# Two small parameter loads of a fused transformer kernel, fetched as single rows and spread to the partitions by TensorE

## The chip, the core and the metric

The kernel runs on one core of one Trainium2 chip. The metric is the device time of one execution in microseconds (us). The core has five instruction streams that matter here: TensorE (PE, with its weight loads shown apart as PEld), VectorE (DVE), ScalarE (ACT), GpSimd (POOL) and SyncE (SP). Every stream runs in order and is tied to the others by semaphores. SP and ACT also issue DMA transfers, which 16 DMA engines carry out; in the profile SP's queue is q1 and ACT's is q10.

## What is computed

Two layers over x of shape (4, 256, 256) and a context of shape (4, 256, 128). Each layer adds a gated cross attention and then a gated feed-forward part:

```python
x = x + tanh(g_xattn[0]) * L0_xattn(layernorm(x), ctx)      # the part that the change touches
x = x + tanh(g_ffn[0])   * L0_ffn(layernorm(x))             # ternary weights, 8-bit activations
x = x + tanh(g_xattn[1]) * L1_xattn(layernorm(x), ctx)      # 16 heads
x = x + tanh(g_ffn[1])   * L1_ffn(layernorm(x))             # 64 experts, top 8

def L0_xattn(logits, features):
    query = features @ Wq.T + bq                            # bq, bk: 128 values each
    key = features @ Wk.T + bk
    attention = softmax(query @ key.T)
    return attention-weighted sum of logits
```

`bq` and `bk` are the first layer's biases. The four values of `g_xattn` and `g_ffn` are the gates. All of them are float32.

## The kernel before

The 1024 tokens lie as 8 tiles of 128, or as 4 batches of 256. Everything fits in SBUF, the order of the work is written out by hand for each engine, and a tile of one batch moves from engine to engine by semaphores. The first layer's attention goes through these functions, all within the first 40 us:

- SP issues the loads in the order of lines 302 to 321: the transposed context `ctxT_raw` (512 KB), the weights `wqk0` (128 KB; the profile prints `wqk`), `x` in two halves of 512 KB, the gate weights, and so on.
- ACT issues two loads at its start: `bqk` (line 1582, 128 partitions of 8 bytes) and `gains_raw` (line 1583, 128 partitions of 16 bytes; the host has copied the four gates into 128 rows). Both count on semaphore `l_small`.
- PE begins with `warm()` (lines 748 to 753): eight matmuls of a matrix of ones into PSUM bank 4 that nobody reads, then waits for `ctxT_raw` and `wqk0`. `query_key` (line 744) follows four times: one float32 matmul 128x128 by 128x512 each, which the profile shows as two passes, so that line 744 has eight. `energy` (line 759) multiplies query and key of a batch, `turn_rows_0` (723) and `turn_att` (767) transpose, `mix` (777) applies the attention.
- ACT copies each `query_key` result from PSUM to `qkA` with the bias added (`copy_qk`, line 1385; it waits for `l_small` in the first call), and `gates()` (line 1555) takes the tanh of the gates between the third and the fourth copy. Then come the exponentials (`exp_A`, 1391).
- DVE begins with `stats_0` (lines 1880 and 1883) on the first half of x, then takes the row maxima of the energies (`max_A`, line 1906), and normalises the exponentials (`norm_A`, 1910 and 1912).
- POOL writes the constants, splits the context (`low_ctxT`, 566), and normalises x (516).

`hs` is a scratch tile of the first feed-forward part. Its first writer is `abs_gate` (line 1559). PSUM bank 3 is first used by `energy(2, 3)`. `sum_abs` (line 784) is a later stage of PE with matmuls that load a full 128x128 float32 weight and stream one column.

Of the kernel before, what the change touches and what calls it, by code (L numbers as in the profile page):

```python
# [9 lines left out]
ACT = mybir.ActivationFunctionType  # L10
AX = mybir.AxisListType

P = 128
# [24 lines left out]
def flamingo_kernel(nc, x_tok, ctx_tok, ctxT, qk0, bias0, gains, gate_wT, down_wT, down_tail,  # L38
                    norm_g1, norm_g2, gqk, head_qk, head_vo, router_w, expert_w, shared_w,
                    shared_down, outT, w_rows):  # L40
    with ExitStack() as ctx:
        def sb(name, shape, dt=F32):
            return ctx.enter_context(nc.sbuf_tensor(name, shape, dt))

        def sem(name):
            return ctx.enter_context(nc.semaphore(name))

        pairs = [ctx.enter_context(nc.psum_tensor(f"bank{2 * i}", [P, 2, 512], F32)) for i in range(4)]
        bank = [pairs[i // 2][:, i % 2, :] for i in range(8)]
# [8 lines left out]
        ones = sb("ones", [P, P])  # L58
# [6 lines left out]
        ctxT_lo = sb("ctxT_lo", [P, TOK], F32R)  # L65
        ctx_hi = sb("ctx_hi", [P, TILES, CDIM], F32R)
        ctx_lo = sb("ctx_lo", [P, TILES, CDIM], F32R)
        gains_raw = sb("gains_raw", [P, 4])
        tg = sb("tg", [P, 4])
        spare = sb("spare", [P, 1])  # L70

# [5 lines left out]
        xnT_hi = sb("xnT_hi", [P, KH, TOK], F32R)  # L77
        xnT_lo = sb("xnT_lo", [P, KH, TOK], F32R)

        bqk = sb("bqk", [P, 2])  # L80
        nmA = sb("nmA", [P, BATCH, 2])
        sumA = sb("sumA", [P, BATCH, 2])
        invA = sb("invA", [P, BATCH, 2])
# [43 lines left out]
        l_ctxT, l_ctx, l_qk0, l_small = (sem(n) for n in ("l_ctxT", "l_ctx", "l_qk0", "l_small"))  # L127
# [5 lines left out]
        l_exp = [sem(f"l_exp{i}") for i in range(4)]  # L133
        pool_const = sem("pool_const")
        g_ctx = sem("g_ctx")
        a_ctx, a_tg = sem("a_ctx"), sem("a_tg")

        v_link = sem("v_link")
# [10 lines left out]
        def link_g(pool, ins):  # L149
# [11 lines left out]
        t_qkA, a_qkA, t_eA, v_mA, a_eA, v_nA, t_aA, a_aA, t_oA, v_xA = (sem(n) for n in (  # L161
            "t_qkA", "a_qkA", "t_eA", "v_mA", "a_eA", "v_nA", "t_aA", "a_aA", "t_oA", "v_xA"))
# [6 lines left out]
        def sf(name, shape, dt=F32):  # L169
            return bctx.enter_context(nc.sbuf_tensor(name, shape, dt))  # L170
# [13 lines left out]
        hs = sf("hs", [P, 4, INTER])  # L184
# [2 lines left out]
        hT = sf("hT", [P, 2, KI, P], BF16)  # L187
        down_t = sf("down_t", [P, KI, HID], BF16)
        bctx.close()
        silu_g, h_raw = hs[:, 0:2, :], hs[:, 2:4, :]  # L190
        flat = w2[:, :, :].rearrange("p i n -> p (i n)")
        qkA = flat[:, 0:2 * TOK].rearrange("p (i n) -> p i n", i=2)
# [82 lines left out]
        def bank4(i):  # L275
            return bank[i][:, :].rearrange("p (a n) -> p a n", a=2)
# [440 lines left out]
        def _(pe):  # L717
# [29 lines left out]
            def warm():  # L747
                pe.wait_ge(pool_const, 2)
                for _ in range(8):
                    pe.matmul(bank[4][:, 0:P], ones[:, :], ones[:, :], start=True, stop=True)  # L750
                pe.wait_ge(pool_const, 5)
                pe.wait_ge(l_ctxT, 16)
                pe.wait_ge(l_qk0, 16)
# [226 lines left out]
            def experts_down(par, slot, t, s, start=False):  # L980
# [5 lines left out]
                mm.then_inc(t_D, 1)  # L986

            warm()
            query_key(0, 0, 2)
            query_key(1, 0, 5)  # L990
# [380 lines left out]
        def _(act):  # L1371
# [9 lines left out]
            def copy_qk(i, h, k, bk):  # L1381
                act.wait_ge(t_qkA, k + 1)
                if k == 0:
                    act.wait_ge(l_small, 32)
                act.activation(qkA[:, i, h * 512:(h + 1) * 512], bank[bk][:, :], ACT.Identity,
                               bias=bqk[:, i:i + 1]).then_inc(a_qkA, 1)

            def exp_A(b, bk):
                act.wait_ge(v_mA, b + 1)
# [159 lines left out]
            def high_ctxT():  # L1549
                act.wait_ge(l_ctxT, 16)  # L1550
                act.activation(ctxT_hi[:, :], ctxT_raw[:, :], ACT.Copy).then_inc(a_ctx, 1)

            def gates():
                act.wait_ge(l_small, 32)
                act.activation(tg[:, :], gains_raw[:, :], ACT.Tanh).then_inc(a_tg, 1)

            def abs_gate(k):
                act.wait_ge(l_gate[k], 16)
# [20 lines left out]
            def load_table(function):  # L1579
                act.activation(spare[:, :], tg[:, 0:1], function)  # L1580

            act.dma_start(bqk[:, :], bias0).then_inc(l_small, 16)
            act.dma_start(gains_raw[:, :], gains).then_inc(l_small, 16)
            high_ctxT()
            copy_qk(0, 0, 0, 2)
            copy_qk(1, 0, 1, 5)
            copy_qk(0, 1, 2, 7)
            gates()
            copy_qk(1, 1, 3, 2)
            exp_A(0, 6)  # L1590
# [283 lines left out]
        def _(dve):  # L1874
            T = tinyB

            def tile_stats(i0, i1):

                for i in range(i0, i1):
                    ins = dve.bn_stats(stats[:, i, :], x[:, i, :])  # L1880
                link(dve, ins)
                for i in range(i0, i1):
                    ins = dve.bn_aggr(mv[:, i, :], stats[:, i, :])
                return ins
# [15 lines left out]
            def stats_0(b):  # L1900
                dve.wait_ge(l_x[b // 2], 16)
                tile_stats(2 * b, 2 * b + 2).then_inc(v_pw1, 1)

            def max_A(b, bk):
                dve.wait_ge(t_eA, b + 1)
                dve.tensor_reduce(nmA[:, b, :], bank4(bk), AX.X, ALU.max, negate=True).then_inc(v_mA, 1)
# [269 lines left out]
            def key_gain():  # L2176
                dve.wait_ge(l_gqk, 16)
                dve.tensor_scalar(gk[:, :], gqk_raw[:, 0:1], gqk_raw[:, 1:2], float(D) ** -0.5, ALU.mult,
                                  ALU.mult).then_inc(v_gk, 1)

            stats_0(0)
            stats_0(1)
            max_A(0, 6)
            max_A(1, 1)
            max_A(2, 3)
            norm_A(0)
            stats_0(2)
# [411 lines left out]
```

## Time and profile before

| | before |
|---|---|
| median of 3 runs | 620.29 us |
| lowest, highest | 620.06, 620.79 us |
| the profiled execution's own time | 620.25 us |
| its span, first to last instruction | 618.5 us |
| outside the span | 1.75 us |
| PE, PEld, DVE, ACT, POOL busy | 98, 85, 78, 68, 38% of the span |

The profile is of one execution. Times in it count from the start of its span. A row of the timeline gives start, duration, engine, line, operation, tiles and shapes, and in square brackets how long the engine had been idle and what released it. A PE row's duration goes from the start of a pass to its modelled end, and passes overlap, so that the distance between two starts is what a pass costs in a row of passes. The chain of work that ended last is followed back from the last instruction, each piece to what released it.

### The profile page before, as it was taken

To read this page: it belongs to the slowest core of one execution; us is meant where nothing else is said; L and a number is where in the kernel's file an instruction comes from. 1 tells how busy PE (TensorE), PEld (TensorE's weight loads), DVE (VectorE), ACT (ScalarE), POOL (GpSimd) and SP (SyncE) were. 2 spreads that over 40 slices of the span, in tenths; PEclk is the share of its full clock that TensorE was granted. 3 is DMA by queue.
4 is the path that set the end of the run, shared out by engine and by line. 5 is a ranking of instruction groups with operands and counts; after the bars stand their busy time and mean duration, and the time that the engine had idled before them with its cause. 6 is when DMAs were issued, how large, how long until landed. Compare 5 with 4: busy or idle time off the path is not lost.

```text
span 618.5 us, 11618 instructions
## 1 busy us (share of the span) xinstructions
PE 605.6 (98%) x3644; PEld 524.2 (85%) x3644; DVE 482.0 (78%) x1139; ACT 422.2 (68%) x1080; POOL 233.8 (38%) x280
## 2 busy tenths in 40 slices
PE   8889999999999999999999999999999999999997
PEld 6657899999999999999998888888887888887886
DVE  4999889888777687788775787778877677777776
ACT  6998998988888888889898444364444444443442
POOL 5899798666666666556662020000000000000000
PEclk9999999999999999999999999999999999999999
DMA  8503221000000000000030445443756466554630
GB/s 294 198 26 103 78 77 37 17 1 2 2 2 2 2 2 2 1 2 1 6 125 2 140 159 147 150 149 100 214 166 171 113 171 166 165 154 148 199 128 34
DMA packets 33653, 56.47 MB, mean 91 GB/s; under 512 B 12800, under 2 KB 13504, under 8 KB 33600
## 3 DMA queue, kind: packets, MB, share of 16 engines
q1 hardware_dynamic: 33312, 55.82, 29.6%
q8 instruction: 26, 0.43, 0.3%
q14 instruction: 27, 0.22, 0.1%
q10 hardware_dynamic: 288, 0.00, 0.0%
HBM read 53.45 MB, written 1.31 MB: 89 GB/s over the span
## 4 chain that ended last, share of the span: by engine, by line
PE 87%; DVE 6%; issue 2%; POOL 2%; ACT 2%; DMA 1%; SPq 0%; DVEq 0%; ACTq 0%; POOLq 0%
PE bank L296 24%; PE bank L298 24%; PE bank L297 24%; PE bank L897 4%; PE bank L872 2%; PE bank L864 2%; PE bank L938 1%; PE bank L824 1%; ACT att L1489 1%; DVE hs L1974 1%; PE bank L817 1%; DMA wqk<-in_qk 1%; PE bank L797 1%; PE bank L744 1%; PE bank L777 1%
## 5 line engine op out<-in xcount | busy, mean ns | idle before, releaser
L1537 ACT ACTIVATE inter_hi<-inter 128x512 fp32r<-128x512 f32 x63 | 39.8, 632 | 140.6 <-DVE inter L2165 140.6
L296 PE MATMUL bank<-xnT_hi,front_hi 128*128 128x512 f32 (+1 forms) x260 | 102.0, 392 | 0.0
L298 PE MATMUL bank<-xnT_hi,front_lo 128*128 128x512 f32 (+1 forms) x260 | 101.7, 391 | 0.0
L297 PE MATMUL bank<-xnT_lo,front_hi 128*128 128x512 f32 (+1 forms) x260 | 101.7, 391 | 0.0
L2169 DVE TENSOR_TENSOR inter_lo<-inter,inter_hi 128x512 fp32r<-128x512 f32 x63 | 43.6, 692 | 37.5 <-ACT inter_hi L1537 37.0
L1489 ACT ACTIVATE att<-bank,shift,rq 128x256 f32<-128x256 f32 x128 | 71.3, 572 | 1.9 <-DVE shift L2055 1.9
L557 POOL TENSOR_TENSOR att<-att,rowinv 128x512 f32<-128x512 f32 x60 | 62.9, 1064 | 12.1 <-DVE rowinv L2065 12.1
L2138 DVE TENSOR_TENSOR prod<-gate_s,bank 128x512 f32<-128x512 f32 x63 | 43.2, 686 | 22.0 <-PE bank L298 20.0
L2048 DVE TENSOR_REDUCE rowmax<-bank 128x2 f32<-128x512 f32 x64 | 43.5, 684 | 20.7 <-PE bank L298 20.3
L297 PEld LDWEIGHTS bank<-xnT_lo,front_hi 128*128 128x128 f32 x260 | 48.9, 188 | 11.3
L298 PEld LDWEIGHTS bank<-xnT_hi,front_lo 128*128 128x128 f32 x260 | 48.8, 188 | 11.3
L296 PEld LDWEIGHTS bank<-xnT_hi,front_hi 128*128 128x128 f32 x260 | 48.8, 188 | 11.1
L541 POOL TENSOR_TENSOR rk<-msq,minus_half 128x4 f32<-128x4 f32 x32 | 32.8, 1024 | 67.3 <-DVE msq L2037 67.3
L296 PE MATMUL bank<-inter_hi,front_hi 128*128 128x512 f32 (+1 forms) x130 | 51.2, 394 | 0.0
L297 PE MATMUL bank<-inter_lo,front_hi 128*128 128x512 f32 (+1 forms) x130 | 51.0, 392 | 0.0
L298 PE MATMUL bank<-inter_hi,front_lo 128*128 128x512 f32 (+1 forms) x130 | 51.0, 392 | 0.0
L2165 DVE TENSOR_TENSOR inter<-prod,w_all 128x512 f32<-128x512 f32 x63 | 43.6, 692 | 3.6 <-DVE prod L2138 1.8
L2060 DVE TENSOR_TENSOR attT_lo<-bank,attT_hi 128x512 fp32r<-128x512 f32 x64 | 43.1, 681 | 3.3 <-ACT attT_hi L1478 2.9
L296 PE MATMUL bank<-m_all,o_hi 128*128 128x256 f32 x128 | 38.9, 304 | 0.7 <-DVE o_lo L2075 0.6
L1478 ACT ACTIVATE attT_hi<-bank 128x512 fp32r<-128x512 f32 x64 | 35.6, 603 | 4.5 <-PE bank L897 4.4
L1533 ACT ACTIVATE gate_s<-bank 128x512 f32<-128x512 f32 x63 | 37.0, 587 | 2.2 <-PE bank L298 2.0
L296 PE MATMUL bank<-kh,qh 128*128 128x256 f32 x128 | 36.7, 287 | 0.1
(270 smaller groups left out, 1816.5 us busy)
## 6 DMA issues: line engine op xcount, KB each, us to landing
w_all<-w_rows SPq DMA_DIRECT2D x128, 128.0 KB, 2.9
raw<-in_expert_w SPq DMA_DIRECT2D x32, 384.0 KB, 3.5
wvo_raw<-in_expert_w SPq DMA_DIRECT2D x16, 384.0 KB, 3.6
e_more<-in_expert_w SPq DMA_DIRECT2D x16, 384.0 KB, 3.6
raw<-in_head_qk SPq DMA_DIRECT2D x8, 384.0 KB, 3.4
wvo_raw<-in_head_vo SPq DMA_DIRECT2D x4, 384.0 KB, 3.0
w_keep<-in_head_vo SPq DMA_DIRECT2D x4, 384.0 KB, 3.3
gate_raw<-in_gate_wT SPq DMA_DIRECT2D x2, 704.0 KB, 9.0
```

The lines of the kernel that those rows point to most:

```text
L296: pe.matmul(out, l_hi, r_hi_, start=start, stop=False, skip_group_check=True)
L297: pe.matmul(out, l_hi, r_lo_, start=False, stop=False, skip_group_check=True)
L298: return pe.matmul(out, l_lo, r_hi_, start=False, stop=stop, skip_group_check=True)
L557: pool.tensor_tensor(a, a, rowinv[:, n % 2, h, :].unsqueeze(2).broadcast_to([P, 2, SEQ]), ALU.mult).then_inc(g_att, 1)
L1489: act.activation(att[:, n % 2, h, t, :], bank4(SBK[h])[:, t, :], ACT.Exp, bias=shift[:, n % 2, h, t:t + 1], scale=rq[:, n % 4, t * 2 + h:t ...
L1533: act.activation(gate_s[:, slot, :], bank[GB][:, :], ACT.Silu).then_inc(a_silu, 1)
L1537: act.activation(inter_hi[:, slot, :], inter[:, slot, :], ACT.Copy).then_inc(a_Ihi, 1)
L2048: dve.tensor_reduce(rowmax[:, n % 2, h, :], bank4(SBK[h]), AX.X, ALU.max, negate=True).then_inc(v_max, 1)
L2060: dve.tensor_tensor(attT_lo[:, h, :, :], bank4(TBK[h]), f(attT_hi[:, h, :, :]), ALU.subtract).then_inc(v_Tlo, 1)
L2138: dve.tensor_tensor(prod[:, slot, :], gate_s[:, slot, :], bank[UB][:, :], ALU.mult).then_inc(v_mul1, 1)
L2165: dve.tensor_tensor(inter[:, slot, :], prod[:, slot, :], w_all[:, par, :], ALU.mult).then_inc(v_mul2, 1)
L2169: dve.tensor_tensor(inter_lo[:, slot, :], inter[:, slot, :], f(inter_hi[:, slot, :]), ALU.subtract).then_inc(v_Ilo, 1)
```

## The change

The biases are fetched as one row of 256 values into the first partition of `hs`, the gates as one row of four values behind it. PE gets three matmuls in `warm()`, behind the eight of ones and a wait for `l_small`: two take every second value of the bias row as weights of one partition by 128 columns and a single 1.0 as the moving operand, which puts 128 bias values into a column of bank 3; the third takes one partition of ones as weights and the four gates as the moving operand, which puts them into four columns of all partitions. DVE gets a copy of the six columns to a new tile `small` as its first instruction. ACT's `copy_qk` and `gates()` read `small` and wait for that copy by a new semaphore `v_small`.

```diff
-        gains_raw = sb("gains_raw", [P, 4])
+        small = sb("small", [P, 6])
-        bqk = sb("bqk", [P, 2])
+        t_small, v_small = sem("t_small"), sem("v_small")
+        bias_row, gain_row = hs[0:1, 0, 0:2 * P], hs[0:1, 0, 2 * P:2 * P + 4]
         (in warm, behind the eight matmuls of ones)
+                pe.wait_ge(l_small, 32)
+                for i in range(2):
+                    pe.matmul(bank[3][:, i:i + 1], bias_row.rearrange("o (p i) -> o i p", i=2)[:, i, :],
+                              ones[0:1, 0:1], start=True, stop=True, skip_group_check=True)
+                pe.matmul(bank[3][:, 2:6], ones[0:1, :], gain_row, start=True, stop=True,
+                          skip_group_check=True).then_inc(t_small, 1)
                 pe.wait_ge(pool_const, 5)
                 pe.wait_ge(l_ctxT, 16)
                 pe.wait_ge(l_qk0, 16)
         (in copy_qk)
                 if k == 0:
-                    act.wait_ge(l_small, 32)
+                    act.wait_ge(v_small, 1)
                 act.activation(qkA[:, i, h * 512:(h + 1) * 512], bank[bk][:, :], ACT.Identity,
-                               bias=bqk[:, i:i + 1]).then_inc(a_qkA, 1)
+                               bias=small[:, i:i + 1]).then_inc(a_qkA, 1)
         (in gates)
-                act.wait_ge(l_small, 32)
-                act.activation(tg[:, :], gains_raw[:, :], ACT.Tanh).then_inc(a_tg, 1)
+                act.wait_ge(v_small, 1)
+                act.activation(tg[:, :], small[:, 2:6], ACT.Tanh).then_inc(a_tg, 1)
         (ACT's first two instructions)
-            act.dma_start(bqk[:, :], bias0).then_inc(l_small, 16)
-            act.dma_start(gains_raw[:, :], gains).then_inc(l_small, 16)
+            act.dma_start(bias_row, bias0.rearrange("(o p) i -> o (p i)", o=1)).then_inc(l_small, 16)
+            act.dma_start(gain_row, gains[0:1, :]).then_inc(l_small, 16)
         (DVE)
+            def keep_small():
+                dve.wait_ge(t_small, 1)
+                dve.tensor_copy(small[:, :], bank[3][:, 0:6]).then_inc(v_small, 1)
+            keep_small()
             stats_0(0)
```

## Rows read from the trace of the kernel before

**Rows 1.** The page: busy time of each engine, the granted clock by slices, the chain.
```profile
PE 605.6 (98%) x3644; PEld 524.2 (85%) x3644; DVE 482.0 (78%) x1139; ACT 422.2 (68%) x1080; POOL 233.8 (38%) x280
PEclk9999999999999999999999999999999999999999
PE 87%; DVE 6%; issue 2%; POOL 2%; ACT 2%; DMA 1%; SPq 0%; DVEq 0%; ACTq 0%; POOLq 0%
```

**Rows 2.** The chain that ended last, first 14 us: start us, us, piece.
```profile
0.73 0.40 SPq L302
1.18 4.05 DMA wqk<-in_qk
5.23 0.14 issue
5.37 3.90 PE bank L744 x8
9.27 2.60 PE bank L759 x12
11.89 0.69 DVE nmA L1906
```

**Rows 3.** The timeline of 0 to 6.8 us, the engines' rows around the change.
```profile
1.14 3.78 PE L750 MATMUL bank<-ones 128*128 128x128 f32 x16 [1.14 <-POOL minus_magic L437]
...
4.92 1.06 ACT L1551 ACTIVATE ctxT_hi<-ctxT_raw 128x1024 fp32r<-128x1024 f32 x1 [1.98 <-DMA ctxT_raw<-in_ctxT]
...
5.37 3.90 PE L744 MATMUL bank<-ctxT_raw,wqk 128*128 128x512 f32 x8 [0.45 <-DMA wqk<-in_qk]
...
6.73 0.69 ACT L1385 ACTIVATE w<-bank,bqk 128x512 f32<-128x512 f32 x1 [0.75 <-PE bank L744]
```

**Rows 4.** Timeline of PE from 4.5 us, of PEld from 5 us.
```profile
4.50 0.42 PE L750 MATMUL bank<-ones 128*128 128x128 f32 x1
```
```profile
5.34 0.50 PEld L744 LDWEIGHTS bank<-ctxT_raw,wqk 128*128 128x128 f32 x2 [0.72 <-issue]
6.10 0.19 PEld L744 LDWEIGHTS bank<-ctxT_raw,wqk 128*128 128x128 f32 x1 [0.26 <-issue]
6.53 0.19 PEld L744 LDWEIGHTS bank<-ctxT_raw,wqk 128*128 128x128 f32 x1 [0.24 <-issue]
```

**Rows 5.** Timeline, one float32 matmul of one column (two passes) and its neighbours.
```profile
21.97 0.30 PEld L784 LDWEIGHTS bank<-absum,ones 128*128 128x128 f32 x2
...
22.08 0.28 PE L784 MATMUL bank<-absum,ones 128*128 128x1 f32 x2
22.22 1.19 PE L931 MATMUL bank<-ctxT_hi 128*128 128x512 f32 x4
```

**Rows 6.** DMA issues at the start: size each, us from issue to landing.
```profile
ctxT_raw<-in_ctxT SPq DMA_DIRECT2D x1, 512.0 KB, 4.2
...
bqk<-in_bias ACTq DMA_DIRECT2D x1, 1.0 KB, 4.0
gains_raw<-in_gains ACTq DMA_DIRECT2D x1, 2.0 KB, 4.2
```

**Rows 7.** Timeline: the issue of the second small load; queue q10, 2 to 5 us.
```profile
1.18 0.45 ACTq L1583 DMA_DIRECT2D gains_raw<-in_gains x1
```
```profile
q10 hardware_dynamic: 288, 0.00, 5.3%
```

**Rows 8.** Busy time by stretch: PE, PEld, DVE, ACT, POOL, then PEclk, DMA share, GB/s.
```profile
3.00:3.50 0.50, 0.50 (x4) 0.50 (x4) 0.00 (x0) 0.00 (x0) 0.00 (x0) 1.00 0.79 287
...
8.00:9.00 1.00, 1.00 (x3) 0.39 (x3) 0.91 (x4) 0.83 (x2) 0.49 (x1) 1.00 1.02 425
...
30.00:40.00 10.00, 7.55 (x48) 5.68 (x49) 9.79 (x20) 8.96 (x23) 8.08 (x9) 1.00 0.14 41
...
60.00:618.50 558.50, 553.42 (x3356) 486.12 (x3356) 432.92 (x1019) 371.00 (x975) 186.55 (x203) 1.00 0.28 84
```

**Rows 9.** Timeline, 8 to 14 us: who holds up DVE and PE there.
```profile
8.05 0.75 DVE L1880 BATCH_NORM_STATS2 stats<-x 128x6 f32<-128x256 f32 x2 [8.05 <-DMA x<-in_x_tok]
...
9.76 0.25 DVE L1883 BATCH_NORM_AGGREGATE mv<-stats 128x2 f32<-128x6 f32 x2
...
10.17 0.69 DVE L1906 TENSOR_REDUCE nmA<-bank 128x2 f32<-128x512 f32 x1 [0.16 <-PE bank L759]
...
13.36 0.66 PE L767 MATMUL bank<-ident,w 128*128 128x128 f32 x4 [1.03 <-DVE w L1912]
```

**Rows 10.** Timeline: a DVE instruction on a PSUM column; ACT's first use of loaded gate weights.
```profile
18.12 0.16 DVE L1955 TENSOR_SCALAR wsc<-bank 128x1 f32<-128x1 f32 x1 [0.27 <-PE bank L784]
```
```profile
14.55 1.42 ACT L1559 ACTIVATE hs<-gate_raw 128x1408 f32<-128x1408 f32 x1
```

## The prediction

> **What bounds the kernel now.** I read the page first. PE is busy 98% of the span and holds 87% of the chain [rows 1], so that nothing outside PE's order is worth much by itself. The change, however, touches only the first 10 us. There the question is not which engine is busiest but which wait ends last. The chain in order of time answers that [rows 2]: it starts with SP's issues, rides on the transfer of `wqk` until 5.23 us, enters PE with `query_key` (line 744, 3.90 us), goes on with `energy` (line 759) and reaches DVE's maxima at 11.89 us. The small loads are not on it. ACT's first bias copy began at 6.73 us because PE had finished its matmul then, not because the bias came [rows 3].
>
> Next I looked at what happens if the start slips or comes forward. From 30 to 40 us DVE is busy 9.79 of 10 us, and behind 60 us PE is busy 553.42 of 558.50 us [rows 8]. No transfer times the stages behind the start: ACT's `abs_gate` at 14.55 us shows no idle time before it [rows 10]. So I take it that a shift of `query_key` goes into the end one to one, and that it is the only thing that can.
>
> **The change part by part.** The sum is made against the profiled execution, 620.25 us with 618.5 us of span; it lies 0.04 us under the median of the three runs (620.29), so no correction is needed.
>
> (1) *The loads.* `bqk` and `gains_raw` are issued at 0.74 and 1.18 us and land 4.0 and 4.2 us later [rows 6, 7], at 4.7 and 5.4 us. ACT's queue shows 288 packets which took 5.3% of 16 engines' time over the 3 us from 2 to 5 us [rows 7], which is 0.16 us for each engine. That is the lower bound of what removing them frees. The upper bound comes from the rate: 287 GB/s while they are under way, 425 GB/s later [rows 8]. The 640 KB of `ctxT_raw` and `wqk0` at 425 GB/s need 1.5 us, at 287 they need 2.2 us, so `wqk` could land up to 0.7 us earlier if all of that difference were their doing (the start-up of the queues has its part in it, so I take 0.2 us). Both ends are worth nothing by themselves if PE isn't ready, see (3). The same holds for x: the first half starts DVE at 8.05 us, and DVE is through with its two statistics at 10.01 us and then waits 0.16 us for PE's energy [rows 9]. An earlier x only lengthens that wait.
>
> (2) *When the rows are there.* No transfer of one row is in the trace. The nearest are the small loads themselves. At the latest they land where the 128 packets of the second did, 1.18 + 4.2 = 5.38 us; at the earliest only the issue time, 1.2 us, is a firm limit. With one data packet in place of 128 a row has hardly any turns to wait for beside the big transfers, and I take both to be landed before 4.5 us, when PE starts its last pass of ones [rows 4].
>
> (3) *PE's three matmuls.* This is the term that decides. They stand in front of `query_key` in PE's order. Each float32 matmul is two passes, so six passes, each with a weight load of 128 columns, though only one partition is filled. The 16 passes of ones go from 1.14 to 4.50 us, start of first to start of last: 3.36 / 15 = 0.224 us a pass [rows 3, 4]. This is the lower clock level: a pass of 512 columns later takes 0.43 us (6.10 to 6.53) [rows 4], so 128 columns should cost 0.107 at the 2.4 GHz level and 0.213 at 1.2 GHz. (The granted clock in the rows prints 1.00 from the start [rows 8]; I go by the durations.) At the high level a matmul of one column costs 0.07 a pass hidden behind others (22.08 to 22.22 us for two) and 0.15 by its loads (0.30 for two) [rows 5]. For six passes that gives 0.42 us at the least, 0.9 us at the high level by the loads, and 1.34 us at 0.224. The clock is still low at 4.7 us, so I take 0.224, the nearest row in time and in weight shape. The last pass of ones gives way at 4.50 + 0.22 = 4.72 us, and `query_key` starts at 4.72 + 1.34 = 6.07 us in place of 5.37.
>
> The Trainium skill speaks on this in "TensorE: Matmul & The Clock Gate", section "LDWEIGHTS (loading the stationary operand)": the time of a weight load goes with its columns and not with the rows filled, 128 columns at 1.2 GHz or 107 ns. That is a rule against this change, since using one partition saves nothing. With its figure the six passes would be 0.64 us, `query_key` would start at 5.36 us and the change would cost nothing, as an estimate from the page; the trace has 0.15 to 0.22 us for a float32 load and decides.
>
> (4) *What of that is given back by the clock.* Before, the first pass of line 744 lasts from 5.37 to 6.10 us, where the next ones take 0.43 [rows 4]. At half speed it would need 0.85. So the clock rose within it: with t us at half speed, t/0.85 + (0.73 - t)/0.43 = 1 gives t = 0.6, a rise at about 5.98 us. If it rises at the same moment, the late `query_key` runs at full speed from its first pass. Its second pass starts at 6.07 + 0.43 = 6.50 us in place of 6.10: a delay of 0.40 us, not 0.70.
>
> (5) *The hop over DVE.* The last small pass ends at about 5.84 + 0.25 = 6.1 us, then a DVE instruction on a few PSUM columns takes 0.16 us [rows 10]; with a hand-over on either side `small` is there at 6.4 us. ACT needs it when the first `query_key` is through, 6.73 + 0.40 = 7.1 us. DVE has nothing queued behind the new wait that could run before x lands at 8.05 us [rows 9]. So the hop costs nothing, with 0.7 us of cover on ACT and 1.6 us on DVE; if the small matmuls ended later, `query_key` would move with them and the cover on ACT would stay.
>
> (6) *ACT's issues* remain two, its table load and its wait for the context until 4.92 us [rows 3] hide them. The copy of the bias reads as many bytes as before. All this is zero.
>
> Sum: -0.0 (loads, hidden behind PE) + 0.40 (PE) + 0 (DVE, ACT) = +0.4 us; 620.25 + 0.4 = 620.65, rounded to 620.7 us. The bounds of (3) and (2): with 0.42 us for the six passes `query_key` starts at 5.14 us if the transfer is early enough, runs its first pass at half speed up to the rise (0.84 of the 0.85 us that it needs), and its second starts at 5.99 us: 0.11 us early, giving 620.1. With the rows landing at 5.38 us, the passes begin there, 2.7 of them at 0.224 up to 5.98 us and 3.3 at 0.15, end at 6.48 us, and the second pass of `query_key` comes at 6.91: +0.81, giving 621.1 us.
>
> **The rivals.**
> *The clock rises later (slower).* Before, PE streams full columns from 1.14 us to 4.92, pauses 0.45 us and streams 512 columns until the clock rises near 5.98 us. After, the 1.3 us ahead of that moment hold six weight loads and a dozen moving columns. If this little work keeps the clock down, `query_key` runs at 1.2 GHz from 6.07 us. Each pass costs 0.43 us more; if all eight are slow, 8 x 0.43 = 3.4 us on top of 0.4, 624.1 us. A rise at 9 us costs (9.0 - 6.07) / 2 = 1.5 us, 620.25 + 0.4 + 1.5 = 622.1 us. It turns into slower by over 0.2% when the rise comes later than about 7.7 us: 0.4 + (7.7 - 6.07) / 2 = 1.2. For it speaks that the passes of one column leave the array empty between the loads. Against it speaks that the engine had worked without a break for 3.8 us by then and no longer pauses for 0.45 us, and that PE's wait of 1.03 us at 13.36 us did not bring the clock down: four passes of 128 columns took 0.66 us right behind it [rows 9]. The Trainium skill, same page, section "The HAM clock gate" has activity release the clock and idleness take it back; taken by itself it would have the filled pause help, and no row here shows how a weight load counts. Chance 12%.
> *The transfers were what held the start (faster).* If the small packets cost the two big transfers 0.7 us and the six passes are cheap, `query_key` can start at 5.14 us as above: 620.1 us, a gain, but one within 0.2%. Even if the clock rose with it and all passes came 0.23 us early, it would be 620.0 us. PE's passes of ones end where they do, so that the idle time of 0.45 us is all there is. For more, something behind 60 us would have to fall differently; no row shows what. Chance of a gain over 0.2%: 7%.
> *It doesn't do what it says.* If the row is cut into pieces again or the landing is governed by the big transfers of the other queue, the rows come no earlier than 5.4 us: 621.1 us by the bound above. Part of the forecast's range, 15%.
>
> **How the numbers follow.** A difference of 0.2% is 1.24 us here, about what a measurement of this kernel can tell from no change. My forecast with its bounds (620.1 to 621.1) has 66% and the late rows 15%, both within 0.2%: same 0.81. Slower is the clock rival, 0.12. Faster is the rest, 0.07. The range takes the lower bound of 620.1 less a little for the spread of the runs (620.06 to 620.79), 619.9, and at the upper end reaches into the clock case up to a rise at 9 us, 622.1.
>
> **What would show it.** In the new profile I look for six passes of `warm`'s new lines between 4.7 and 6.1 us without a wait for a DMA before them; the first pass of line 744 near 6.07 us, its distance to the next 0.43 us; DVE's maximum at 10.6 in place of 10.17 us with 0.5 us of idle time before it, released by PE; POOL's and DVE's statistics at 8.0 us or a little sooner; ACT's first bias copy still released by PE and not by DVE. The forecast is wrong if PE waits for the small rows, if the second pass of line 744 still takes 0.7 us or more, if the six passes together take under 0.6 us, or if a slip at 10 us is no longer seen at 60 us.

## The result: two groups of executions, 1.0024 of the time before

| | before | after |
|---|---|---|
| executions | 20 | 19 |
| median | 620.30 us | 622.66 us |
| lowest, highest | 619.88, 621.06 us | 620.45, 623.31 us |
| ratio after / before | | 1.0024, 95% interval 1.0015 to 1.0033 |
| the profiled execution and its span | 620.25, 618.5 us | 622.66, 620.9 us |

(One execution of the changed kernel, of 744.99 us, and one of e4 below, of 852.26 us, had a mean granted clock of 0.755 and 0.656 and are left out; one of e3, of 621.81 us with 0.948, is counted.) The median says little here, because nothing lies near the middle: nine executions are at 620.45 to 620.93 us and ten at 622.66 to 623.31 us. The profiled one is of the upper group. By the ratio the change costs 1.5 us.

The page of the changed kernel, busy time of the engines, answers to [rows 1]:

```profile
PE 608.4 (98%) x3650; PEld 526.2 (85%) x3650; DVE 482.4 (78%) x1140; ACT 422.0 (68%) x1080; POOL 233.8 (38%) x280
```

The chain that ended last, first 15 us (start us, us, piece), answers to [rows 2]. The transfer of `wqk` is gone from it. Behind POOL's constants it runs in PE's own order:

```profile
1.14 3.78 PE bank L751 x16
4.92 0.94 PE bank L754 x4
5.86 0.43 PE bank L756 x2
6.29 5.11 PE bank L745 x8
11.40 2.60 PE bank L766 x12
14.03 0.69 DVE nmA L1917
```

Line 745 is `query_key` (744 before), 5.11 us in place of 3.90. Its weight loads in the timeline of PEld, each of which begins when the pass before the one it serves begins, answer to [rows 4]:

```profile
4.85 0.92 PEld L754 LDWEIGHTS bank<-ones,hs 1*128 1x128 f32 x4 [0.23 <-issue]
5.66 0.54 PEld L756 LDWEIGHTS bank<-hs,ones 1*128 1x128 f32 x2
6.21 0.50 PEld L745 LDWEIGHTS bank<-ctxT_raw,wqk 128*128 128x128 f32 x2
7.23 0.34 PEld L745 LDWEIGHTS bank<-ctxT_raw,wqk 128*128 128x128 f32 x1 [0.52 <-issue]
8.08 0.34 PEld L745 LDWEIGHTS bank<-ctxT_raw,wqk 128*128 128x128 f32 x1 [0.52 <-issue]
8.94 0.34 PEld L745 LDWEIGHTS bank<-ctxT_raw,wqk 128*128 128x128 f32 x1 [0.52 <-issue]
9.52 0.19 PEld L745 LDWEIGHTS bank<-ctxT_raw,wqk 128*128 128x128 f32 x1 [0.25 <-issue]
9.95 0.19 PEld L745 LDWEIGHTS bank<-ctxT_raw,wqk 128*128 128x128 f32 x1 [0.24 <-issue]
```

The passes are 0.85 us apart (7.23, 8.08, 8.94), then once 0.58, then 0.43. So the array ran at 1.2 GHz up to a moment between 8.94 and 9.52. With t us of that pass at half speed, t/0.85 + (0.58 - t)/0.43 = 1 gives t = 0.3: the clock rose at 9.24 us. The trace's own record of the granted clock begins at the same 9.24 us; ahead of its first entry the page prints 1.00. In the profile of before this record begins at 5.83 us, a little ahead of the 5.98 of the prediction. There the first pass of line 744 was counted from 5.37 us, but the weight load for the second pass, which begins with the first pass, starts at 5.51. From 5.51 to 6.10 us the same sum is t/0.85 + (0.59 - t)/0.43 = 1 with t = 0.32, and gives 5.83 too.

DVE and ACT behind it, from the timeline, answer to [rows 9] and [rows 3]:

```profile
6.32 0.17 DVE L1913 COPY small<-bank 128x6 f32<-128x6 f32 x1 [6.32 <-PE bank L756]
8.23 0.75 DVE L1887 BATCH_NORM_STATS2 stats<-x 128x6 f32<-128x256 f32 x2 [1.75 <-DMA x<-in_x_tok]
8.33 0.69 ACT L1392 ACTIVATE w<-bank,small 128x512 f32<-128x512 f32 x1 [2.63 <-PE bank L745]
12.30 0.69 DVE L1917 TENSOR_REDUCE nmA<-bank 128x2 f32<-128x512 f32 x1 [2.11 <-PE bank L766]
```

The first maximum starts at 12.30 us in place of 10.17, +2.13 us. `energy` starts 2.14 us later (first the row of before, then the changed kernel's):

```profile
9.10 2.75 PE L759 MATMUL bank<-w 128*128 128x256 f32 x12
```

```profile
11.24 2.75 PE L766 MATMUL bank<-w 128*128 128x256 f32 x12
```

VectorE's instruction at the end of the first layer, line 1904 (1897 before), starts at 61.65 in place of 59.49 (+2.16), and the whole execution takes 2.41 us more. Before and after:

```profile
59.49 0.67 DVE L1897 TENSOR_TENSOR xnT_lo<-bank,xnT_hi 128x512 fp32r<-128x512 f32 x1
```

```profile
61.65 0.67 DVE L1904 TENSOR_TENSOR xnT_lo<-bank,xnT_hi 128x512 fp32r<-128x512 f32 x1
```

### The profile page after: what moved, and what is told of

It reads as the page before. It is cut to its first block, busy times and chain, and to the rows that moved or that the text cites. A ratio compares the mean times of both kernels' runs of the same rounds, so it can differ in the third digit from the quotient of the medians.

```text
span 620.9 us, 11631 instructions
## 1 busy us (share of the span) xinstructions
PE 608.4 (98%) x3650; PEld 526.2 (85%) x3650; DVE 482.4 (78%) x1140; ACT 422.0 (68%) x1080; POOL 233.8 (38%) x280
## 4 chain that ended last, share of the span: by engine, by line
PE 89%; DVE 6%; ACT 2%; issue 2%; POOL 1%; ACTq 0%; DVEq 0%; POOLq 0%
PE bank L297 24%; PE bank L298 24%; PE bank L299 24%; PE bank L904 4%; PE bank L879 2%; PE bank L871 2%; ACT att L1496 1%; PE bank L945 1%; PE bank L831 1%; PE bank L745 1%; DVE hs L1985 1%; PE bank L824 1%; PE bank L804 1%; PE bank L784 1%; PE bank L751 1%
```

## The experiments

Each table row counts executions; before was run beside them on the same chip. The first four (e1 for the first time, e2, e3 and e4) ran on one chip, all later ones on another, on which before itself has more upper executions. "Upper" are those of 621.5 us and more. The ratio is that to before.

| kernel | all | upper | values of the others | values of the upper | ratio, 95% interval |
|---|---|---|---|---|---|
| before, with the result | 20 | 0 | 619.88 to 621.06 | | |
| before, beside the first four | 35 | 1 | 619.70 to 620.95 | 622.90 | |
| before, beside the second four | 35 | 6 | 619.96 to 621.49 | 622.13 to 622.61 | |
| before, beside the last four | 34 | 4 | 619.99 to 621.14 | 622.04 to 622.82 | |
| changed, with the result | 19 | 10 | 620.45 to 620.93 | 622.66 to 623.31 | 1.0024, 1.0015 to 1.0033 |
| changed, again | 12 | 5 | 620.28 to 621.01 | 622.81 to 623.10 | 1.0018, 1.0005 to 1.0031 |
| e1, both times | 23 | 0 | 618.86 to 621.41 | | 1.0007 and 0.9983, see below |
| e2 | 11 | 4 | 620.01 to 620.65 | 622.30 to 622.75 | 1.0010, 0.9997 to 1.0023 |
| e3 | 12 | 5 | 620.38 to 620.93 | 621.81 to 623.57 | 1.0025, 1.0013 to 1.0036 |
| e4 | 10 | 0 | 619.97 to 621.14 | | 1.0005, 0.9996 to 1.0014 |
| e5 | 12 | 8 | 620.11 to 620.59 | 622.36 to 622.79 | 1.0011, 0.9997 to 1.0025 |
| e6 | 12 | 7 | 619.90, 621.14 to 621.37 | 621.50 to 622.75 | 1.0013, 1.0003 to 1.0023 |
| e8 | 12 | 5 | 619.39 to 620.11 | 621.67 to 622.31 | 0.9996, 0.9982 to 1.0010 |
| e10 | 11 | 1 | 619.66 to 620.85 | 621.73 | 0.9998, 0.9989 to 1.0007 |
| e11 | 11 | 0 | 619.21 to 621.00 | | 0.9998, 0.9989 to 1.0007 |
| e12 | 11 | 7 | 621.12 to 621.47 | 621.55 to 622.65 | 1.0020, 1.0011 to 1.0029 |

A profile shows one execution, and here it is often an end of a group: it is the fastest of its kernel in e1 (both times), e3, e6, e11 and the second run of the changed kernel, and the slowest in e2 and e5.

### Which half of the change: e1 and e2

e1, the loads alone:

```diff
-                pe.wait_ge(l_small, 32)
-                (the three small matmuls)
-                dve.wait_ge(t_small, 1)
-                dve.tensor_copy(small[:, :], bank[3][:, 0:6]).then_inc(v_small, 1)
+                dve.wait_ge(l_small, 32)
+                dve.memset(small[:, :], 0.5).then_inc(v_small, 1)
```

> The change's loads alone: biases and gates are fetched as rows, PE has none of the three small matmuls, and VectorE fills the six columns with 0.5 once the rows have landed, so the real biases and gates are left out of the computation. Theory (the clock): in the changed kernel's profile the first three passes of the projection lie 0.85 us apart and later ones 0.43, so the clock rose near 9.2 us in place of 5.98, because of what PE does from 4.85 to 6.2 us. Without the small matmuls PE is as before: all executions near 620.3 us, none at 622 to 623, the weights landing 0.2 us earlier than 5.23 us at most. Rival (the loads shift something else, for instance which transfer comes first): executions at 622 to 623 us here too.

Measured: 620.27 us, ratio 1.0007 (0.9998 to 1.0015), eleven executions between 619.22 and 621.41, none at 622. This is as the theory of the clock expects; the loads alone bring no upper group, which the rival wanted. The weights landed 3.5 us after their issue, at 4.7 us, 0.5 earlier than before where 0.2 was expected. The values spread more than expected.

e2, the matmuls alone, in the kernel before:

```diff
                 for _ in range(8):
                     pe.matmul(bank[4][:, 0:P], ones[:, :], ones[:, :], start=True, stop=True)
+                for _ in range(2):
+                    pe.matmul(bank[3][:, 0:1], ones[0:1, :], ones[0:1, 0:1], start=True, stop=True)
+                pe.matmul(bank[3][:, 0:4], ones[0:1, :], ones[0:1, 0:4], start=True, stop=True)
```

> The loads as before (256 small packets), and behind the eight matmuls of ones three more of the same shapes as the change's, one partition of weights by 128 columns with 1, 1 and 4 moving columns, of ones and read by nobody. The clock theory expects what the changed kernel shows: executions in two groups, near 620.7 and near 622.9 us, and in a profile of the slower group passes of the projection 0.85 us apart up to about 9.2 us. The rival that the loads bring the slower group expects 620.7 us alone.

Measured: two groups, seven at 620.01 to 620.65 us and four at 622.30 to 622.75. The profile fell into the upper one (622.75 us) and shows the same picture as the changed kernel, in PEld's timeline:

```profile
6.21 0.50 PEld L744 LDWEIGHTS bank<-ctxT_raw,wqk 128*128 128x128 f32 x2
7.23 0.34 PEld L744 LDWEIGHTS bank<-ctxT_raw,wqk 128*128 128x128 f32 x1 [0.52 <-issue]
8.08 0.34 PEld L744 LDWEIGHTS bank<-ctxT_raw,wqk 128*128 128x128 f32 x1 [0.52 <-issue]
8.94 0.34 PEld L744 LDWEIGHTS bank<-ctxT_raw,wqk 128*128 128x128 f32 x1 [0.52 <-issue]
9.64 0.19 PEld L744 LDWEIGHTS bank<-ctxT_raw,wqk 128*128 128x128 f32 x1 [0.36 <-issue]
```

With all 256 packets in place, three matmuls that nobody reads are enough for the upper group, in 4 of 11 executions where before has 1 of 35 beside them.

### Is it the slip or what fills it: e4, e3, e5, e8

e4 is the kernel before with `range(11)` in place of `range(8)` in `warm()`.

> The kernel before with eleven full matmuls of ones in place of eight: the same six extra passes in front of the projection, all of 128 partitions by 128 columns. Clock theory: extra 6 x 0.224 us in front of the projection, the rise where it was, 5.9 us, the second pass of the projection at about 6.5 us in place of 6.10: +0.4 us, 620.7 us in all executions. Rival (the slip of the projection by itself, past 5.98 us, costs the slower group, whatever fills the time): two groups, 620.7 and 622.9 us.

Measured: one group, 619.97 to 621.14 us, median 620.56, ratio 1.0005 (0.9996 to 1.0014). The profile, 620.62 us, in PEld's timeline:

```profile
5.79 0.45 PEld L744 LDWEIGHTS bank<-ctxT_raw,wqk 128*128 128x128 f32 x2
6.47 0.19 PEld L744 LDWEIGHTS bank<-ctxT_raw,wqk 128*128 128x128 f32 x1 [0.24 <-issue]
6.90 0.19 PEld L744 LDWEIGHTS bank<-ctxT_raw,wqk 128*128 128x128 f32 x1 [0.24 <-issue]
```

The second pass is at 6.47 us (6.5 expected), 0.37 later than before, and the execution takes 0.37 us more. So in the profiles six full passes ahead of the projection cost 0.4 us as worked out; the ratio of 1.0005 agrees with that, but also with nothing.

e3 keeps the single partition and fills the columns:

```diff
-                    pe.matmul(bank[3][:, i:i + 1], ..., ones[0:1, 0:1], ...)
+                    pe.matmul(bank[3][:, i * P:(i + 1) * P], ..., ones[0:1, :], ...)
-                pe.matmul(bank[3][:, 2:6], ones[0:1, :], gain_row, ...)
+                pe.matmul(bank[3][:, 2 * P:3 * P] (as 32 by 4), ones[0:1, :], gain_row (32 times), ...)
```

> The changed kernel with 128 moving columns in each of the three small matmuls in place of 1, 1 and 4 (the ones and the gates repeated), still one partition of weights; VectorE copies in two pieces. If it is the few streamed columns that keep the clock down, the passes cost about the same 0.22 us each, the rise stays at 5.9 us, and all executions are near 620.7 us. If the single filled partition counts as little work as well, two groups stay, near 620.7 and 622.9 us.

Measured: seven at 620.38 to 620.93, four at 622.80 to 623.57 us and one at 621.81 between them. e5 is the other way round, in the kernel before:

```diff
+                for _ in range(3):
+                    pe.matmul(bank[3][:, 0:1], ones[:, :], ones[:, 0:1], start=True, stop=True)
```

> The kernel before, with three matmuls of ones of 128 partitions by 128 columns of weights and a single moving column each behind the eight: the same six passes, full in partitions, empty in columns. With one filled partition and 128 moving columns there were two groups of executions, with 128 by 128 one group. If the filled partitions decide, one group, 619.9 to 621.2 us. If both a single partition and a single column count as little work, two groups, the upper one near 622.7 us, in a third to a half of the executions.

Measured: four at 620.11 to 620.59, eight at 622.36 to 622.79 us. Its profile is of the upper group (622.79 us) and has the latest rise of all, at about 10.2 us, where the distance of the passes falls from 0.85 to 0.43:

```profile
5.78 0.55 PEld L744 LDWEIGHTS bank<-ctxT_raw,wqk 128*128 128x128 f32 x2
6.84 0.34 PEld L744 LDWEIGHTS bank<-ctxT_raw,wqk 128*128 128x128 f32 x1 [0.52 <-issue]
7.70 0.34 PEld L744 LDWEIGHTS bank<-ctxT_raw,wqk 128*128 128x128 f32 x1 [0.52 <-issue]
8.55 0.34 PEld L744 LDWEIGHTS bank<-ctxT_raw,wqk 128*128 128x128 f32 x1 [0.52 <-issue]
9.40 0.34 PEld L744 LDWEIGHTS bank<-ctxT_raw,wqk 128*128 128x128 f32 x1 [0.52 <-issue]
10.25 0.19 PEld L744 LDWEIGHTS bank<-ctxT_raw,wqk 128*128 128x128 f32 x1 [0.51 <-issue]
10.68 0.19 PEld L744 LDWEIGHTS bank<-ctxT_raw,wqk 128*128 128x128 f32 x1 [0.24 <-issue]
```

Here the projection started no later (5.85 us) than in e4 (5.99; the first weight load for it is at 5.78 and 5.79), and the clock still came late. e4 and e5 have the same passes with the same weights at the same times up to there and differ only in the moving columns, 128 against 1 (and in the PSUM bank that these write, 4 against 3), and they have 0 of 10 and 8 of 12 upper executions. That rules out the slip as the cause and leaves the columns. They ran on different chips; beside e5, before has 6 of 35, still far from 8 of 12. For the single partition the case is weaker: e3 with its five of twelve against e4's none of ten, on one chip, and e3 differs from e4 also by a short pause of the weight loads, see (3) below. e8 is the changed kernel with 128 partitions read, 127 of them zeros:

```diff
+            dve.memset(hs[:, 0, 0:2 * P + 4], 0.0).then_inc(v_small, 1)
+            act.wait_ge(v_small, 1)          (ahead of ACT's two loads)
-                    pe.matmul(bank[3][:, i:i + 1], (hs[0:1, ...]), ones[0:1, 0:1], ...)
+                    pe.matmul(bank[3][:, i:i + 1], (hs[:, ...]), ones[:, 0:1], ...)
                 (the third likewise; ACT's later waits for v_small count one more)
```

> The changed kernel with the rows' tile set to zero by VectorE ahead of the loads, and the three small matmuls taking all 128 partitions (127 of zeros) as weights, with 1, 1 and 4 moving columns. If the partitions read decide over the clock, one group near 620.7 us; if the values or the columns do, two groups as before, 620.7 and 622.9 us. The loads start some 0.3 us later, hidden behind the passes of ones.

Measured: seven at 619.39 to 620.11, five at 621.67 to 622.31 us; two groups, both nearly 1 us lower than expected (ratio 0.9996, 0.9982 to 1.0010). The profile has the weights at 1.18 + 3.4 = 4.6 us and the projection at 5.08. The changed kernel's own profile of the lower group (below) has the projection at 5.27, so that 0.2 us of the gain are there; why it does better by more than that wasn't followed up.

Together: of the kernels with the same six passes more than before (the changed one, e2, e3, e4, e5, e8), the one whose passes are full in partitions and columns has 0 of 10 in the upper group, the others 4 to 8 of 11 or 12 (the changed one 15 of 31). A dozen executions each don't rank the latter among themselves. No single one of e2 and e3 would prove the difference from e4 either; all together (37 of 78 against 0 of 10), and e5 by itself, do.

### Before or behind the rise: e6 and e12

e6 is the changed kernel with `range(6)` in `warm()`, e12 with `range(12)`.

> The changed kernel with six matmuls of ones ahead of the three small ones in place of eight, so that PE is through at 1.14 + 18 x 0.224 = 5.2 us. Clock theory: less full work ahead of the small passes, so the late rise comes in at least as many executions as in the changed kernel (11 of 20); the lower group moves from 620.7 to about 620.3 us, the upper from 622.9 to about 622.5. The rival that the slower group comes from the slip of the projection past 5.98 us expects the upper group to be gone.

Measured: 621.58 us, one execution at 619.90, nine at 621.14 to 621.93, two at 622.64 and 622.75. The rival falls, since leaving the slip out didn't take the later times away (where the projection started in them no profile shows); the two expected groups are not there either, the times fill the stretch between. The profile caught the 619.90, so the middle values have no profile. In it the clock rose during the small passes, at 4.63 us by its record: the weight loads are 0.21 us apart up to 4.54 and 0.11 from 4.71 us on. It also shows when the rows are there, in PEld's timeline:

```profile
4.15 0.74 PEld L754 LDWEIGHTS bank<-ones,hs 1*128 1x128 f32 x4 [0.39 <-DMA hs<-in_gains]
4.82 0.30 PEld L756 LDWEIGHTS bank<-hs,ones 1*128 1x128 f32 x2
5.13 0.30 PEld L745 LDWEIGHTS bank<-ctxT_raw,wqk 128*128 128x128 f32 x2
```

PE waited 0.39 us for the gates' row, until 4.15 us, of the 0.9 us (four passes at 0.224) that two fewer matmuls give. So e6 differs from the changed kernel by this pause too, and not only by the work ahead of the small passes.

> The changed kernel with twelve matmuls of ones ahead of the small ones in place of eight. Clock theory: a late rise needs the small passes to come before the clock has risen; with 24 full passes, up to 6.5 us at the lower level, it has risen by then in nearly all executions, and there is one group, at 621.0 to 622.0 us for the later start of the projection (7.2 to 7.4 us). The rival by which the slip of the projection itself brings the upper group expects all executions above 622.7 us.

Measured: one broad group, 621.12 to 622.65 us, median 621.67, three of eleven above the expected 622.0. No execution is where the rival wants all of them. The profile (621.18 us) has passes of 0.43 us from the start of the projection at 6.28 us:

```profile
5.49 0.54 PEld L754 LDWEIGHTS bank<-ones,hs 1*128 1x128 f32 x4
6.28 0.30 PEld L745 LDWEIGHTS bank<-ctxT_raw,wqk 128*128 128x128 f32 x2
6.81 0.19 PEld L745 LDWEIGHTS bank<-ctxT_raw,wqk 128*128 128x128 f32 x1 [0.24 <-issue]
```

Its clock rose at 4.28 us, as early as in other kernels without the four extra matmuls, so that the profile doesn't show what these do. The times say a little more: a rise at 9.24 us would put an execution near 621.18 + (9.24 - 4.28) / 2 = 623.7 us, as an estimate, and none lies there. So the upper group of the changed kernel seems to go when more full work stands ahead of the small passes, but the spread of 1.5 us isn't explained, and the time is worse all the same.

### What the loads alone are worth: e1 again, e10, e11

> The loads alone once more (real biases and gates left out, 0.5 in their place), for a second profile and for the lower group against the kernel before: 11 executions lay at 619.2 to 620.3 (6) and 620.9 to 621.4 us (5). If its lower group is real, it comes from the weights landing at 4.75 us in place of 5.23 and the projection starting 0.6 us earlier: lower values 0.5 us under those of before. If the upper group is a later rise of the clock, its profile, if it falls there, has passes of the projection 0.85 us apart past 6 us.

Measured: 619.93 us, twelve at 618.86 to 620.16, ratio 0.9983 (0.9973 to 0.9992). The profile (618.86 us), timeline of PEld and DVE, shows the projection 0.6 us and x 1.2 us earlier than before:

```profile
4.72 0.30 PEld L745 LDWEIGHTS bank<-ctxT_raw,wqk 128*128 128x128 f32 x2 [0.20 <-issue]
5.26 0.19 PEld L745 LDWEIGHTS bank<-ctxT_raw,wqk 128*128 128x128 f32 x1 [0.24 <-issue]
6.82 0.75 DVE L1881 BATCH_NORM_STATS2 stats<-x 128x6 f32<-128x256 f32 x2 [2.62 <-DMA x<-in_x_tok]
```

The first time the ratio was 1.0007, the second time 0.9983; the lowest values lie 0.5 and 1.1 us under those of before both times. The upper part of the first time (five at 620.9 to 621.4 us) didn't come back, so that it has no profile.

e10 has the packets, but behind the weights on SP's queue:

```diff
             sp.dma_start(wqk0[:, :, :], qk0).then_inc(l_qk0, 16)
+            sp.dma_start(bqk[:, :], bias0).then_inc(l_small, 16)
+            sp.dma_start(gains_raw[:, :], gains).then_inc(l_small, 16)
-            (the same two on ACT)
```

> The kernel before with the two small loads (256 packets, nothing on PE) issued by SyncE behind the projection's weights in place of by ScalarE beside them. If the small packets held the context and the weights up, these land at 4.7 to 4.8 us as with the rows alone, the projection starts at about 4.8 us, and the executions lie at 619.0 to 620.2 us as there. x comes later than with the rows (6.8 us), near 8 us, and that costs nothing. If what helped with the rows was something else, the executions lie as those of before (619.7 to 621).

Measured: 620.36 us, ratio 0.9998 (0.9989 to 1.0007): the weights land at 1.18 + 3.6 = 4.8 us as expected, the time doesn't follow. The profile shows two new waits, in ACT's waits and DVE's timeline:

```profile
ACT w L1387 <- DMA gains_raw<-in_gains: 1.0, 1, 1.0
```

```profile
9.53 0.25 DVE L1883 BATCH_NORM_AGGREGATE mv<-stats 128x2 f32<-128x6 f32 x2
9.70 1.32 DVE L1906 TENSOR_REDUCE nmA<-bank 128x2 f32<-128x512 f32 x2
```

ACT's first bias copy now waits 1.0 us for the gates, and x lands at 7.83 us, so that DVE is busy with statistics until 9.70 and takes the maxima without any wait for PE. The next bound lies 0.5 us behind the first. e11 below, where ACT has no such wait, runs into the same one: its first maximum starts at 9.74 us, right behind the statistics.

e11 puts biases and gates into one load of 128 packets of 24 bytes:

```diff
-            act.dma_start(bqk[:, :], bias0).then_inc(l_small, 16)
-            act.dma_start(gains_raw[:, :], gains).then_inc(l_small, 16)
+            act.dma_start(small[:, :], bias0).then_inc(l_small, 16)      (bias0 of 6 columns, from the host)
```

> The kernel before with biases and gates side by side in one load of 128 packets of 24 bytes, nothing on PE. Half the packets: if the cost is by packet, the weights land halfway, near 5.0 us, and the executions lie 0.2 us under those of before; if it is by load on the second queue, they land at 4.75.

Measured: 620.45 us, 619.21 to 621.00, ratio 0.9998 (0.9989 to 1.0007). The weights land 3.7 us after issue, 0.3 earlier, as expected; 0.2 us of time can't be told from nothing. None of the kernels that compute everything beats the one before; this one at least lies under the changed kernel on the same chip (median 620.45 against 620.98, and none of eleven in the upper group against five of twelve).

### The changed kernel in the lower group

> The changed kernel once more, for its groups on this chip and, if the profile falls into the lower one, its first 10 us there: rise of the clock at 5 to 6.2 us, second pass of the projection near 6.5 us, time near 620.6 us. In the upper group: passes 0.85 us apart up to 9 to 10 us, time near 622.9 us.

Measured: 620.98 us, ratio 1.0018 (1.0005 to 1.0031), seven at 620.28 to 621.01 and five at 622.81 to 623.10. This profile is of the lower group (620.28 us). Timeline of PEld, and DVE's first maximum:

```profile
4.49 0.54 PEld L754 LDWEIGHTS bank<-ones,hs 1*128 1x128 f32 x4
4.96 0.30 PEld L756 LDWEIGHTS bank<-hs,ones 1*128 1x128 f32 x2
5.27 0.30 PEld L745 LDWEIGHTS bank<-ctxT_raw,wqk 128*128 128x128 f32 x2
5.81 0.19 PEld L745 LDWEIGHTS bank<-ctxT_raw,wqk 128*128 128x128 f32 x1 [0.24 <-issue]
9.87 0.69 DVE L1917 TENSOR_REDUCE nmA<-bank 128x2 f32<-128x512 f32 x1 [0.71 <-PE bank L766]
```

The clock rose still earlier than expected, during the ones: they make way at 4.49 us in place of 4.72. The six small passes take 5.27 - 4.49 = 0.78 us, 0.13 each on average, the projection starts at the moment at which it started before, and the second pass comes at 5.81, ahead of 6.10. The maximum is 0.30 us early (9.87 against 10.17), line 1904 0.27 us early (59.22 against 59.49), yet the execution as a whole is where before is, 620.28 against 620.25 us. Where the 0.3 us are lost behind 60 us wasn't traced.

The record of the granted clock gives the rise in every profile. Kernels without sparse passes ahead of the projection first:

| profile | rise, us | time, us |
|---|---|---|
| before | 5.83 | 620.25 |
| e4 (full passes) | 6.07 | 620.62 |
| e1, first and second | 5.48, 4.37 | 619.22, 618.86 |
| e10, e11 | 4.55, 4.48 | 619.70, 619.21 |
| changed, again; e3; e8 | 4.04, 4.10, 4.10 | 620.28, 620.38, 619.54 |
| e6, e12 | 4.63, 4.28 | 619.90, 621.18 |
| changed; e2; e5 | 9.24, 9.47, 10.22 | 622.66, 622.75, 622.79 |

In the eight profiles with sparse passes, which begin between 4.15 and 5.49 us, the rise is at 4.63 us or earlier, or at 9.24 or later, and never between; in the six without it is at 4.37 to 6.07. This fits a rise that, if it hasn't come by about the time of the sparse passes, is put off until behind 9 us. Why by so much, no run here tests.

## Why the prediction was half right

The forecast was 620.7 us with 622.1 us as the upper end. By the ratio, 620.3 x 1.0024 = 621.8 us, the change lies inside, but on the side to which I had given 12%; the median of 622.66 is outside. The forecast's time is that of one of the two groups (620.45 to 620.93 us), the clock rival's that of the other. That the first fits is partly luck, since the one profile of that group took another path: the forecast has the second pass of line 744 at 6.50 us and the first maximum at 10.6, the profile has them at 5.81 and 9.87 with 620.28 us at the end. The forecast's picture is seen in e4 (6.47 us), not in the changed kernel. Of the signs of being wrong that it lists, one came true in the upper group: the second pass of line 744 takes 0.85 us (7.23 to 8.08).

- **What bounds the kernel.** Right: the slip at 10 us (+2.13) is found at 59.5 us (+2.16) and in the whole (+2.41). The last 0.25 us came behind 60 us.
- **(1) The loads.** The size was off, the worth in this kernel was right. `wqk` landed 3.9 to 4.0 us after issue in the four profiles with 256 packets, 3.4 to 4.0 in the eight with rows, 0 to 0.6 us earlier (and 3.6 and 3.7 in e10 and e11). In the changed kernel PE had not even finished its passes of ones and small matmuls, so nothing of it counted, as predicted. Taken alone it is worth something between 1.0007 and 0.9983.
- **(2) The rows' arrival.** Right, though closer than thought: 4.15 us in e6 against an assumed 4.5 us at the latest.
- **(3) The six passes.** (6.21 - 4.85) / 6 = 0.227 us each against 0.224. Not foreseen was a pause of the weight loads of 0.23 us ahead of the first one, which put it at 4.85 us and not 4.72; e2, which waits for no load there, has it too, e5 with 128 partitions hasn't. A second one lies behind the last small pass: the weight loads are 0.20 us apart from 4.85 to 5.66, but 0.35 from the last of them (5.87) to the projection's first (6.22), where e5 has 0.21. The projection began at 6.22 us, not 6.07. In the other group the six cost 0.78 us, since they ran at the high level. The Trainium skill's rule ("TensorE: Matmul & The Clock Gate", "LDWEIGHTS (loading the stationary operand)") is borne out in what it says on partitions: at the low level the weight loads of one filled partition lie 0.20 us apart (4.85 to 5.66 us for four) and those of 128 in e5 0.21 (4.50 to 5.78 for six). Its 107 ns lie under both, and a little under the 0.12 us seen at the high level (4.49 to 4.96 for four, the changed kernel again).
- **(4) What the clock gives back.** This is the step that failed. "If it rises at the same moment" took one reading of one execution, 5.98 us (5.83 by the clock's record), for a property of the kernel. The profiles of these runs have the rise from 4.04 to 10.22 us, and the very kernel before has 11 of 124 executions in an upper group of its own. The price of the rival was right: for a rise at 9.24 us its sum gives 0.4 + (9.24 - 6.07) / 2 = 2.0 us, plus 0.15 for the later start, 2.1; `energy` came 11.24 - 9.10 = 2.14 us later. Its chance was wrong: 15 of 31 executions, not 12 in 100. What I set against it, work without a break for 3.8 us, said nothing on what the passes behind would do. e4 and e5 together show what did: six passes at the same times with the same weights, full of columns in the one and with a single column in the other, give 0 of 10 and 8 of 12.
- **(5), (6) The hop and ACT.** Right: `small` was copied at 6.32 us in 0.17 us (6.1 and 0.16 predicted), ACT's first copy at 8.33 us was released by PE.
- **The rival of the transfers.** Right that it is capped. That an earlier x "only lengthens the wait" holds as long as PE is late; e10 shows DVE's statistics take the bound over 0.5 us further down.

What stays open: whether the upper group of the kernel before has to do with its pause of 0.45 us in front of the projection. The kernels in which that pause is at most 0.24 us (e1, e10, e11) have 0, 1 and 0 of 23, 11 and 11, against 11 of 124, which is too few to tell from chance, and none of the upper executions of before was profiled. Open too are e6's middle values and why e8's lower group is so low.

## What to carry to other kernels

Work that is put in front of TensorE's clock rise has to be judged by what becomes of the rise and not only by its 0.2 us a pass: the same six passes cost 0.4 us in the profile when full and, in a third to two thirds of the executions, 2.4 us when sparse. If small work must go to TensorE, put it where the clock is already high and the engine waits (there is 1.03 us of waiting at 13.36 us here, where the gates would be early enough, since their first use behind the tanh is at 17.1 us; this wasn't tried), and look at all execution times, not at their median, before you believe a profile. Before you shorten a transfer, find the second bound: in e10 and e11 it stood 0.5 us behind the first, and the first maximum came no earlier than that.

## What the runs showed of the hardware

- The moment at which TensorE's clock rises from 1.2 to 2.4 GHz moved between executions of kernels with the same first 4 us, from 4.04 us (changed kernel, lower group) over 5.83 (before) to 9.24 us (changed kernel, upper group); with the single columns of e5 it came at 10.22. In all three upper profiles (the changed kernel, e2, e5) the passes of 512 columns lay 0.85 us apart up to it, while the granted clock printed 1.00 throughout; the distances of the passes tell, and so does the start of the clock's record in the trace, which agrees with them (9.24 and 5.83 us in the two profiles worked out above).
- Pauses of the weight loads stood where 128-partition weights gave way to one-partition ones and back (0.23 us without a wait in the changed kernel and e2, 0.35 us between loads in place of 0.21 behind them); e5 with 128 partitions throughout has neither.
- Beside two loads of 128 packets of 8 and 16 bytes, the last of the transfers of 640 KB landed 3.9 to 4.0 us after its issue in four profiles, beside two rows 3.4 to 4.0 in eight, so up to 0.6 us earlier, though these packets took only 5.3% of the DMA engines' time in the stretch, 0.16 us on each.
